# One head's relative-position scores in a fused attention stage: rotated queries against a fixed wave table in place of a skew through DRAM

## The chip, the core and the metric

The kernel runs on 1 core of one Trainium2 chip. Its engines are PE (TensorE, matrix products into PSUM), DVE (VectorE), ACT (ScalarE), POOL (GpSimd) and SP (SyncE, which here only issues DMAs). The metric is the device time of one execution in microseconds. A profiled execution gives the trace that is read below.

## What is computed

Sixteen images of 128 channels x 1024 places go through a convolution block, an attention with relative positions, and a mixture of experts. The change touches the attention alone:

```
pe = positional_encoding(S, D)                    # sin / cos of place * rate, 1024 x 128
q, k, v = (x @ W + b).reshape(B, S, H, dh)        # H = 4 heads, dh = 32
p = (pe @ Wpos).reshape(S, H, dh)
content_score = einsum('bshd,bthd->bhst', q + u_bias, k)
pos_score = rel_shift(einsum('bshd,thd->bhst', q + v_bias, p))
attn = softmax((content_score + pos_score) / sqrt(D))
out = reshape(einsum('bhst,bthd->bshd', attn, v)) @ Wout + bout

rel_shift: pad one column of zeros on the left of each S x S matrix,
           read it as (S+1) x S, drop the first row, read it as S x S
```

The shift makes row s of the position scores a copy of its unshifted row that is moved by 1023 - s places; what falls off comes from row s + 1. Within a tile of 128 query rows each row is moved by another amount.

## The kernel before

The program runs phase after phase: convolution, projection (which writes `queries`, `keys` and `values` to DRAM, each split in a high and a low part), attention, experts, and a last sum. `attention_phase` is written out by hand for each engine: five instruction queues, bound by semaphores. There is no scheduler.

An image (n) is 32 **steps** (s = 0 to 31): 8 tiles of 128 query rows, in each the 4 heads. Step s is head s % 4 of tile s // 4. Each engine goes through `slot(n, b, s)` for every step and does in it its part for this step and for some earlier ones:

- PE: `position_rows` (L1184) fills the PSUM tile `wide_ps` with 1152 columns for step s (L1173 in the trace, 3 or 4 products of up to 512 columns); `content` (L1197) fills `score_ps` for step s-5 (L1201); `turn_weights` (L1205) transposes the weights of step s-6 into `turn_ps` (L1209); every fourth step `sum_values` (L1212, at s % 4 = 2, L1219 in the trace) and the output product (s % 4 = 3, L1250).
- ACT: copies `wide_ps` to one of four `rows` tiles (L943), and takes the exponential of step s-5 in place in `skewed` (L952).
- SP: writes `rows` to DRAM (`skew_dram`, L840), and two steps later reads it back with a row pitch that is one element shorter (L849) into one of eight `skewed` tiles. This pair is the shift.
- DVE: adds `score_ps` to the shifted rows of step s-5 and takes the minimum (L1093, "reduce" below), copies `turn_ps` of step s-6 to one of eight `turned` tiles (L1101), and every fourth step scales the context (L1068), adds to `x` (L1076) and takes reciprocals (L1083, L1085).

`score_ps`, `wide_ps` and `turn_ps` are single buffers.

Beside image n runs the **routing** of image n-1 for the experts: PE transposes `x` and then the normed rows into the spare columns of `wide_ps` ahead of `position_rows` at steps 9 to 11 and 18 to 20 (`fill`, L1154), gating products at 21 (L1163) and places at 27 (L1157 to L1159); DVE does the gating at steps 22 to 25 and 28; POOL takes the root (L893), norms eight tiles (L898) and copies them (L902), which the fill of step 18 waits for (`normed`), and at the end issues 16 indirect DMAs in a row, which scatter the rows to the experts (L907). POOL has no part of the steps of image n.

## Time and profile before

| | us |
|---|---|
| median of 3 runs | 3765.72 |
| lowest, highest | 3761.39, 3768.57 |
| profiled execution, first to last instruction (span) | 4014.9 |
| first and last copy of `wide_ps` in the attention | 1316.6, 3341.0 |

The page gives no other time of the profiled execution than its span. Busy shares of the span: PE 80%, DVE 68%, ACT 55%, POOL 18%; the hardware DMA queue 70.7% of the 16 DMA engines. In the page's 40 slices the attention covers slices 14 to 34, with DMA at 8 to 9 tenths and 308 to 370 GB/s in most of them. The columns of the windows are the stretch, its length, the busy time of each engine with its count of instructions, the mean granted clock of PE as a share of full speed, the DMA share and GB/s. In a timeline a row is start, duration, engine, line, operation, out<-in, and in brackets the idle time before it with what ended it. "remote" is a releaser that the trace does not name.

### The profile page before, as it was taken

To read this page: it belongs to the slowest core of one execution; us is meant where nothing else is said; L and a number is where in the kernel's file an instruction comes from. 1 tells how busy PE (TensorE), PEld (TensorE's weight loads), DVE (VectorE), ACT (ScalarE), POOL (GpSimd) and SP (SyncE) were. 2 spreads that over 40 slices of the span, in tenths; PEclk is the share of its full clock that TensorE was granted. 3 is DMA by queue.
4 is the path that set the end of the run, shared out by engine and by line. 5 is a ranking of instruction groups with operands and counts; after the bars stand their busy time and mean duration, and the time that the engine had idled before them with its cause. 6 is when DMAs were issued, how large, how long until landed. Compare 5 with 4: busy or idle time off the path is not lost. (4 is left out here: it accounts for less than half of the span.)

```text
span 4014.9 us, 76711 instructions
## 1 busy us (share of the span) xinstructions
PE 3223.9 (80%) x29428; PEld 2425.6 (60%) x29428; DVE 2717.7 (68%) x5210; ACT 2196.9 (55%) x3568; POOL 704.4 (18%) x760
## 2 busy tenths in 40 slices
PE   4788888888566788878888888888887885799993
PEld 2556556556454576666666666667665764687772
DVE  4777877876443576668666867667666865577763
ACT  2555545545343575556655665556655652577760
POOL 1000000000001001120212112120212012466660
PEclk9899999999777898889888988888888987899995
DMA  2445545544487998899888988899888983577768
GB/s 55 143 130 176 170 119 163 181 124 167 172 292 254 323 370 309 312 322 341 315 308 313 361 314 314 306 327 345 312 304 312 354 307 129 200 236 240 238 201 335
DMA packets 290943, 1023.22 MB, mean 255 GB/s; under 512 B 51620, under 2 KB 57520, under 8 KB 281574
## 3 DMA queue, kind: packets, MB, share of 16 engines
q1 hardware_dynamic: 273382, 985.62, 70.7%
q0 software_dynamic: 17280, 33.87, 2.3%
q8 instruction: 176, 2.88, 0.3%
q14 instruction: 105, 0.86, 0.1%
HBM read 486.25 MB, written 489.85 MB: 243 GB/s over the span
## 5 line engine op out<-in xcount | busy, mean ns | idle before, releaser
L952 ACT ACTIVATE att_skewed<-att_skewed,att_neg_max 128x1024 f32<-128x1024 f32 x512 | 588.9, 1150 | 422.2 <-DVE att_neg_max L1093 419.3
L943 ACT ACTIVATE att_rows<-att_wide_ps 128x1152 f32<-128x1152 f32 x512 | 573.5, 1120 | 378.1 <-remote 240.5
L1209 PE MATMUL att_turn_ps<-att_ident,att_skewed 128*128 128x128 f32 x4096 | 610.4, 293 | 174.8 <-ACT att_skewed L952 124.2
L1209 PEld LDWEIGHTS att_turn_ps<-att_ident,att_skewed 128*128 128x128 f32 x4096 | 491.1, 150 | 370.7 <-ACT att_skewed L952 284.6
L1093 DVE CUSTOM_DVE_ANT_0 att_skewed<-att_score_ps,att_skewed 128x1024 f32<-128x1024 f32 x512 | 625.3, 1221 | 128.5 <-issue 120.1
L1101 DVE COPY att_turned<-att_turn_ps 128x1024 f32<-128x1024 f32 x512 | 624.9, 1221 | 22.4 <-PE att_turn_ps L1209 19.5
L1173 PE MATMUL att_wide_ps<-att_ps,att_qs 98*128 98x128 f32 (+3 forms) x1920 | 454.2, 358 | 32.8 <-DVE att_token L985 16.5
L1201 PE MATMUL att_score_ps<-att_ks,att_qs 96*128 96x512 f32 x1024 | 383.9, 458 | 28.9 <-DVE att_neg_max L1093 23.0
L907 POOL DMA_INDIRECT expert_rows<-att_expert_rows,att_place x256 | 247.4, 966 | 817.3 <-DVE att_place L1051 730.4
L1173 PEld LDWEIGHTS att_wide_ps<-att_ps,att_qs 98*128 98x128 f32 x1920 | 324.1, 208 | 92.3 <-issue 51.8
L1219 PE MATMUL att_tail_ps<-att_turned,att_vals 128*32 128x128 f32 x8192 | 315.7, 289 | 69.1 <-issue 66.5
L152 POOL DMA_INDIRECT expert_parts<-exp_parts,exp_rows x284 | 300.4, 1058 | 195.4 <-ACT exp_parts L183 129.4
L1219 PEld LDWEIGHTS att_tail_ps<-att_turned,att_vals 128*32 128x32 f32 x8192 | 240.5, 116 | 130.6 <-issue 126.0
L170 ACT ACTIVATE exp_hid<-exp_hid_ps,exp_weights 128x512 f32<-128x512 f32 x284 | 197.3, 695 | 133.5 <-PE exp_hid_ps L249 84.9
L1068 DVE TENSOR_TENSOR att_context<-att_tail_ps,att_recip_t 128x128 f32<-128x128 f32 x128 | 37.0, 289 | 314.6 <-remote 239.0
L1898 PE MATMUL conv_tile<-conv_stacked,conv_tap_products 128*32 128x252 f32 (+1 forms) x4608 | 223.0, 351 | 18.9 <-DMA conv_stacked<-conv_qp 18.9
L210 DVE CAST exp_hidh<-exp_hid 128x512 fp32r<-128x512 f32 x284 | 124.2, 437 | 135.5 <-ACT exp_hid L170 85.9
L1898 PEld LDWEIGHTS conv_tile<-conv_stacked,conv_tap_products 128*32 128x32 f32 x4608 | 162.5, 110 | 82.4 <-DMA conv_stacked<-conv_qp 19.3
L1201 PEld LDWEIGHTS att_score_ps<-att_ks,att_qs 96*128 96x128 f32 x1024 | 168.7, 206 | 65.6 <-DVE att_neg_max L1093 47.3
L214 DVE TENSOR_TENSOR exp_hidl<-exp_hid,exp_hidh 128x512 fp32r<-128x512 f32 x284 | 193.7, 682 | 0.0
L893 POOL TENSOR_TENSOR att_rstd<-att_var,att_minus_half 128x8 f32<-128x8 f32 x16 | 26.8, 1674 | 906.7 <-DVE att_var L1006 906.7
L1683 DVE SCALAR_TENSOR_TENSOR conv_x<-conv_x,conv_taps 128x1024 f32<-128x1024 f32 x128 | 164.5, 1285 | 4.6
(263 smaller groups left out, 5307.4 us busy)
## 6 DMA issues: line engine op xcount, KB each, us to landing
skewed_rows<-att_rows SPq DMA_DIRECT2D x512, 576.0 KB
att_skewed<-skewed_rows SPq DMA_DIRECT2D x512, 512.0 KB
expert_rows<-conv_pad SPq DMA_DIRECT2D x144, 520.0 KB, 11.0
exp_weights<-split_weights SPq DMA_DIRECT2D x71, 1028.0 KB
att_qs<-queries SPq DMA_DIRECT2D x192, 128.0 KB
att_ks<-keys SPq DMA_DIRECT2D x192, 128.0 KB
exp_rows<-expert_rows SPq DMA_DIRECT2D x71, 260.0 KB
sum_part<-expert_parts SPq DMA_DIRECT2D x32, 512.0 KB, 9.5
```

The lines of the kernel that those rows point to most:

```text
L152: pool.indirect_dma_start(parts_dram, bass.IndirectOffsetOnAxis(ap=index, axis=0), parts[b % NY][:, t, :], None, bounds_check=bound, oob_i ...
L170: act.activation(hid[:, g % NF, :], hid_ps[:, g % NH, :], ACT.Gelu, bias=bias_of(b, m)).then_inc(gelu_done, 1)
L907: pool.indirect_dma_start(rows_dram, bass.IndirectOffsetOnAxis(ap=place[k][:, t:t + 1], axis=0), expert_rows[k][:, t, :], None).then_inc(s ...
L943: act.activation(rows[s % ROWS][:], wide_ps[:, 0:WIDE], ACT.Copy).then_inc(wide_read, 1)
L952: act.activation(skewed[r % RING][:], skewed[r % RING][:], ACT.Exp, bias=neg_max[:, k:k + 1], scale=-1.0, accum_out=sums[:, k:k + 1]).then ...
L1093: dve.tensor_tensor_reduce(skewed[r % RING][:], score_ps[:], skewed[r % RING][:], -SCALE, 3.0e38, ALU.add, ALU.min, neg_max[:, k:k + 1]).t ...
L1101: dve.tensor_copy(turned[r % (2 * HEADS)][:], turn_ps[:]).then_inc(turn_read, 1)
L1173: ins = pe.matmul(bank_of[:, a:b], left, right, start=(first[a // HALF] == j), stop=(last[a // HALF] == j), skip_group_check=True)
L1201: last = pe.matmul(score_ps[:, c:c + HALF], qs[b][0:STACK, h, i * P:(i + 1) * P], ks[b][:, h, c:c + HALF], start=True, stop=True)
L1209: last = pe.transpose(turn_ps[:, t * P:(t + 1) * P], skewed[r % RING][:, t * P:(t + 1) * P], ident[:])
L1219: last = pe.matmul(tail_ps[h * DH:(h + 1) * DH, 0:P], vals[b][:, t, h, :], turned[first + h][:, t * P:(t + 1) * P], start=(t == 0), stop=( ...
L1898: last = pe.matmul(to[a * DH:(a + 1) * DH, 0:(end - rows) * WS], tap_products[:, t, a, :], stacked[:, a, rows + dy:end + dy, dx:dx + WS], ...
```

## The change

Head 0 leaves the path through DRAM. Since a sine or cosine at place a - b is a rotation of the one at a by an angle that belongs to b, the 128 rows of a tile can each be rotated by their own angle, and then multiplied with one table of waves that is the same for all rows.

- **Waves.** Once for each image, at steps 26 and 27 of the image before, PE multiplies head 0's queries with its rows of Wpos, and with these with sine and cosine exchanged, 1026 columns each, into `wide_ps` (`waves`); DVE multiplies each with a table of angles (`turn_wave`), the second into `z`; POOL adds the two at step 28 (`turn_rows`). The next fill of `wide_ps` waits for DVE (`wave_read`).
- **Each tile of head 0.** ACT makes a high part of the rotated queries (3 steps ahead), POOL the low part (2 steps ahead); PE computes 1152 columns of three products (high x high, high x low, low x high) with 128 rows instead of one product with 98; ACT copies them to one of two `direct` tiles; POOL masks the own block and the 128 columns behind, adds the two blocks and moves two columns (`mask`), and DVE waits for that (`direct_ready`) in place of the DMA.
- **DMA.** 24 pairs of write and read for each image instead of 32; three `rows` and six `skewed` tiles. Five `turned` tiles instead of eight.
- **POOL.** It now follows the steps. The root is at step 14, norming at step 16 behind the mask of that step, and the scatter is two indirect DMAs in each of eight steps, 29 to 31 of one image and 0 to 4 of the next.
- **Setup.** Four more loads, splits of the wave table and of the weights on DVE, and one round of waves ahead of the first step.

```
+            def scatter(m, t):
+                if t == 0:
+                    pool.wait_ge(normed, 2 * m + 2)
+                    pool.wait_ge(placed, m + 1)
                 for k in range(2):
-                    for t in range(TT):
-                        pool.indirect_dma_start(rows_dram, bass.IndirectOffsetOnAxis(ap=place[k][:, t:t + 1], axis=0),
-                                                expert_rows[k][:, t, :], None).then_inc(scattered, 16)
-
-            for m in range(NB):
-                route_rows(m)
+                    pool.indirect_dma_start(rows_dram, bass.IndirectOffsetOnAxis(ap=place[k][:, t:t + 1], axis=0),
+                                            expert_rows[k][:, t, :], None).then_inc(scattered, 16)
+
+            def turn_rows(n, b):
+                pool.wait_ge(wave_read, 2 * n + 2)
+                pool.tensor_tensor(rotated[b][:, :, 0:P + 1], rotated[b][:, :, 0:P + 1], crossed, ALU.add).then_inc(rotated_ready, 1)
+            def mask(n, s):
+                i = s // HEADS
+                G = TT * n + i
+                to, beyond = direct[G % 2], direct[G % 2][:, T:T + P]
+                mask_chain.begin(pool, G)
+                pool.wait_ge(wide_read, STEPS * n + s + 1)
+                mask_chain.step(pool.tensor_tensor(beyond, beyond, after_mask[:], ALU.mult))
+                mask_chain.step(pool.tensor_tensor(to[:, i * P:(i + 1) * P], to[:, i * P:(i + 1) * P], own_mask[:], ALU.mult))
+                ins = pool.tensor_tensor(to[:, i * P + 2:(i + 1) * P], to[:, i * P + 2:(i + 1) * P], beyond[:, 0:P - 2], ALU.add)
...
+            def slot(n, b, s):
+                if s < STEPS and s % HEADS == 0:
+                    mask(n, s)
+                ahead = first_ahead(n, b, s, LOW_LEAD)
+                if ahead:
+                    rotated_low(*ahead)
+                if s == TURN_ROWS_AT and not is_last(n):
+                    turn_rows(n + 1, 1 - b)
+                at = routed(n, b, s)
+                if at and at[2] == STATS_AT + 4:
+                    root(at[0])
+                if at and at[2] == OFFSET_AT + 1:
+                    route_rows(at[0])
+                if at and at[2] >= SCATTER_AT and not is_last(at[0]):
+                    scatter(at[0], at[2] - SCATTER_AT)
...
+            def turn_wave(n, b, k):
+                dve.wait_ge(wave_filled, 2 * n + k + 1)
+                to = crossed if k else rotated[b][:, :, 0:P + 1]
+                dve.tensor_tensor(to, wave_tiles, angles[:, k, :].unsqueeze(1).broadcast_to((P, TT, P + 1)), ALU.mult).then_inc(wave_read, 1)
...
                 at_least(pe, wide_read, STEPS * n + s)
+                if s - 1 in WAVES_AT and not is_last(n):
+                    pe.wait_ge(wave_read, 2 * n + 3 + WAVES_AT.index(s - 1))
                 if spared:
                     fill(*spared)
                 turn = (i + 1) * P
...
+                else:
+                    pe.wait_ge(rot_low_ready, TT * n + i + 1)
+                    pieces = [(c, d, 0, T - i * P + c) for c, d in by_bank(0, turn)]
+                    pieces += [(c, d, 1, c - i * P) for c, d in by_bank(turn, T)] + [(T, WIDE, 1, 2)]
+                    products = []
+                    for c, d, k, at in pieces:
+                        high_part, low_part = rot_high[i % 2][:, k:k + P], rot_low[i % 2][:, k:k + P]
+                        products += [(c, d, high_part, wave_high[:, at:at + d - c]), (c, d, high_part, wave_low[:, at:at + d - c]),
+                                     (c, d, low_part, wave_high[:, at:at + d - c])]
...
+                if s in WAVES_AT and not is_last(n):
+                    if s == WAVES_AT[0]:
+                        pe.wait_ge(first_loaded[1 - b], uses(n + 1, 1 - b, FIRST))
+                    pe.wait_ge(wide_read, STEPS * n + s + 1)
+                    waves(n + 1, 1 - b, WAVES_AT.index(s))
```

**PE around steps 26 to 28 of image 0.** `att_vals` marks the values of step 26, `att_context` the output product of step 27. Before:

```order
775 L1219 MATMUL att_tail_ps<-att_turned,att_vals 32x128 x32
776 L1173 MATMUL att_wide_ps<-att_ps,att_qs 128x512
777 L1173 MATMUL att_wide_ps<-att_ps,att_qs 128x384
778 L1173 MATMUL att_wide_ps<-att_ps,att_qs 128x128 x2
779 L1201 MATMUL att_score_ps<-att_ks,att_qs 128x512 x2
780 L1209 MATMUL att_turn_ps<-att_ident,att_skewed 128x128 x8
781 L1250 MATMUL att_tail_ps<-att_context,att_wout 128x128
782 L1173 MATMUL att_wide_ps<-att_ps,att_qs 128x512 x2
783 L1173 MATMUL att_wide_ps<-att_ps,att_qs 128x128
784 L1201 MATMUL att_score_ps<-att_ks,att_qs 128x512 x2
```

The same place of the program now, where the wave products stand behind the values and behind the output product (L1361), and the last rows are the start of step 28 (head 0):

```order
841 L1361 MATMUL att_wide_ps<-att_qs,att_w_wave 128x2
842 L1323 MATMUL att_wide_ps<-att_ps,att_qs 128x512
843 L1323 MATMUL att_wide_ps<-att_ps,att_qs 128x384
844 L1323 MATMUL att_wide_ps<-att_ps,att_qs 128x128 x2
845 L1368 MATMUL att_score_ps<-att_ks,att_qs 128x512 x2
846 L1376 MATMUL att_turn_ps<-att_ident,att_skewed 128x128 x8
847 L1416 MATMUL att_tail_ps<-att_context,att_wout 128x128
848 L1361 MATMUL att_wide_ps<-att_qs,att_w_wave 128x512 x2
849 L1361 MATMUL att_wide_ps<-att_qs,att_w_wave 128x2
850 L1323 MATMUL att_wide_ps<-att_wave_high,att_rot_high 128x512
851 L1323 MATMUL att_wide_ps<-att_wave_low,att_rot_high 128x512
852 L1323 MATMUL att_wide_ps<-att_wave_high,att_rot_low 128x512
```

Each run of three wave products is an extra use of `wide_ps`, between two position fills.

**DVE in steps 26 and 27 of image 0** (L1236 is the reduce, L1244 the copy of the turned weights, which stand there before as well, as L1093 and L1101), now:

```order
537 L1244 COPY att_turned<-att_turn_ps 128x1024
538 L1199 TENSOR_TENSOR att_rotated<-att_wide_ps,att_angles 128x8x129
539 L1207 TENSOR_TENSOR att_context<-att_tail_ps,att_recip_t 128x128
540 L1235 MEMSET att_marker 128x1
541 L1236 ISA att_skewed,att_neg_max<-att_score_ps,att_skewed 128x1024
542 L1236 ISA att_neg_max 128x1
543 L1244 COPY att_turned<-att_turn_ps 128x1024
544 L1199 TENSOR_TENSOR att_z<-att_wide_ps,att_angles 128x8x129
545 L1215 SCALAR_TENSOR_TENSOR att_x<-att_tail_ps,att_bias_out,att_x 128x128
```

The two rows L1199 are new; each stands behind the copy of its step.

**POOL, from one root to the next.** Before, with the whole routing of one image in four groups:

```order
44 L893 TENSOR_TENSOR att_rstd<-att_var,att_minus_half 128x8
45 L898 TENSOR_SCALAR att_expert_rows<-att_z,att_rstd,att_offset 128x128 x8
46 L902 COPY att_expert_rows<-att_expert_rows 128x8x128
47 L907 DMA expert_rows<-att_expert_rows,att_place 147456x130 x16
```

Now, from the root of step 14 to the norming of step 16, and the scatter from step 29 on:

```order
102 L947 TENSOR_TENSOR att_rstd<-att_var,att_minus_half 128x8
103 L984 TENSOR_TENSOR att_direct<-att_direct,att_after_mask 128x128
104 L985 TENSOR_TENSOR att_direct<-att_direct,att_own_mask 128x128
105 L986 TENSOR_TENSOR att_direct<-att_direct 128x126
106 L989 COPY att_direct<-att_direct 128x2
107 L954 ISA
108 L954 TENSOR_SCALAR att_expert_rows<-att_z,att_rstd,att_offset 128x128 x8
...
125 L970 TENSOR_TENSOR att_rotated<-att_rotated,att_z 128x8x129
126 L965 DMA expert_rows<-att_expert_rows,att_place 147456x130 x2
127 L975 TENSOR_TENSOR att_rot_low<-att_rotated,att_rot_high 128x129
128 L965 DMA expert_rows<-att_expert_rows,att_place 147456x130 x4
129 L984 TENSOR_TENSOR att_direct<-att_direct,att_after_mask 128x128
```

The mask of step 16 now stands ahead of the norming, and the 16 indirect DMAs are cut into pieces with masks and low parts between them.

## Rows read from the trace of the kernel before

**Rows 1.** The page's head: the profiled execution.
```profile
span 4014.9 us, 76711 instructions
```

**Rows 2.** Windows: an image without its end, a stall, a whole image (columns above).
```profile
core 0: us, PE busy (x) PEld busy (x) DVE busy (x) ACT busy (x) POOL busy (x), PEclk, DMA share, GB/s
1920.40:1938.00 17.60, 8.26 (x33) 3.90 (x32) 0.00 (x0) 0.13 (x2) 11.48 (x12) 0.56 0.43 164
1940.80:2048.00 107.20, 95.96 (x962) 76.36 (x965) 88.06 (x197) 74.00 (x109) 9.17 (x13) 0.94 0.99 355
```

**Rows 3.** Timelines of PE, DVE and POOL in a stall; POOL's first and last of 16.
```profile
1923.71 1.09 PE L1219 MATMUL att_tail_ps<-att_turned,att_vals 128*32 128x128 f32 x5 [0.86 <-issue]
1938.05 0.29 DVE L1068 TENSOR_TENSOR att_context<-att_tail_ps,att_recip_t 128x128 f32<-128x128 f32 x1 [17.66 <-remote]
1915.22 1.08 POOL L907 DMA_INDIRECT expert_rows<-att_expert_rows,att_place  x1 [49.23 <-DVE att_place L1051]
1934.28 0.96 POOL L907 DMA_INDIRECT expert_rows<-att_expert_rows,att_place  x1 [0.30 <-issue]
```

**Rows 4.** Waits: who waited for whom, us in total, times, longest.
```profile
ACT att_rows L943 <- remote: 240.5, 13, 18.7
DVE att_marker L1092 <- DMA att_skewed<-skewed_rows: 99.1, 72, 3.8
```

**Rows 5.** ACT's copies: starts of tiles 4, 5, 7 and the next image; image 8's last tile.
```profile
1991.95 1.11 ACT L943 ACTIVATE att_rows<-att_wide_ps 128x1152 f32<-128x1152 f32 x1
2006.89 1.12 ACT L943 ACTIVATE att_rows<-att_wide_ps 128x1152 f32<-128x1152 f32 x1
...
2039.85 1.11 ACT L943 ACTIVATE att_rows<-att_wide_ps 128x1152 f32<-128x1152 f32 x1
...
2069.76 1.13 ACT L943 ACTIVATE att_rows<-att_wide_ps 128x1152 f32<-128x1152 f32 x1
...
2426.37 1.11 ACT L943 ACTIVATE att_rows<-att_wide_ps 128x1152 f32<-128x1152 f32 x1
...
2439.37 1.11 ACT L943 ACTIVATE att_rows<-att_wide_ps 128x1152 f32<-128x1152 f32 x1
```

**Rows 6.** Timelines of PE and DVE through one undisturbed tile of image 5.
```profile
1950.24 0.84 PE L1173 MATMUL att_wide_ps<-att_ps,att_qs 98*128 98x128 f32 x4
1952.45 0.78 PE L1173 MATMUL att_wide_ps<-att_ps,att_qs 98*128 98x256 f32 x4
1953.07 0.68 PE L1201 MATMUL att_score_ps<-att_ks,att_qs 96*128 96x512 f32 x2
1954.21 1.09 PE L1209 MATMUL att_turn_ps<-att_ident,att_skewed 128*128 128x128 f32 x8 [0.46 <-ACT att_skewed L952]
1959.65 1.09 PE L1209 MATMUL att_turn_ps<-att_ident,att_skewed 128*128 128x128 f32 x8 [0.54 <-ACT att_skewed L952]
1962.56 0.81 PE L1173 MATMUL att_wide_ps<-att_ps,att_qs 98*128 98x256 f32 x4
1951.64 1.22 DVE L1093 CUSTOM_DVE_ANT_0 att_skewed<-att_score_ps,att_skewed 128x1024 f32<-128x1024 f32 x1 [0.97 <-issue]
1954.19 1.22 DVE L1093 CUSTOM_DVE_ANT_0 att_skewed<-att_score_ps,att_skewed 128x1024 f32<-128x1024 f32 x1
1957.09 1.22 DVE L1093 CUSTOM_DVE_ANT_0 att_skewed<-att_score_ps,att_skewed 128x1024 f32<-128x1024 f32 x1
```

**Rows 7.** Timelines: POOL's norming, PE's fill that needs it, and a DVE product with PSUM.
```profile
1992.09 3.46 POOL L898 TENSOR_SCALAR att_expert_rows<-att_z,att_rstd,att_offset 128x128 f32<-128x128 f32 x8 [4.38 <-DVE att_offset L1058]
1995.76 0.52 PE L1154 MATMUL att_wide_ps<-att_ident,att_expert_rows 128*128 128x128 f32 x3
1100.94 1.21 DVE L579 TENSOR_TENSOR proj_zl<-proj_z_ps,proj_zh 128x1024 fp32r<-128x1024 f32 x1
```

**Rows 8.** DMA issues: the two transfers of the shift.
```profile
skewed_rows<-att_rows SPq DMA_DIRECT2D x512, 576.0 KB
att_skewed<-skewed_rows SPq DMA_DIRECT2D x512, 512.0 KB
```

239 lines of the change are left out of this document (177 added, 62 removed).

## The prediction

> **What bounds the kernel now.** Three views, in this order: the windows and the waits, to split the attention in kinds of stretches; ACT's copies of `wide_ps`, one for each step, as a clock of the program; and the timelines of PE and DVE through one tile, to see which chain sets its length.
>
> The first thing to see is a stall that comes once for each routed image. While POOL issues its 16 indirect DMAs in a row (from 1915.22 to 1935.2), PE gets its instructions in driblets, DVE sits 17.66 us, DMA falls to 0.43 [rows 2, 3]. It makes the last tile of an image 29.9 us (2039.85 to 2069.76) where image 8, whose stall comes later, has 13.0 [rows 5]: 16.9 us, in 15 images 254 us. 13 of them show as ACT waits of together 240.5 us [rows 4]. Now the span is 4014.9 [rows 1], and 4014.9 - 254 = 3761, which is the timed median within 5 us. I read this as a stall that only the profiled execution has. The sum is therefore made against the span without it, 3761, and carried over to 3765.7; the other reading is a rival below.
>
> Image 5 runs from 1940.8 (the window's start) to 2069.76, 129.0 us, less the stall 112 [rows 2, 5]. An undisturbed tile takes 12.32 (PE's fills at 1950.24 and 1962.56, [rows 6]). What sets it is a chain: reduce of step 0 (1954.19), exponential, reciprocal, reduce of step 1 (1957.09), exponential, transposes (1959.65), values, fill of step 3 (1962.56), content, reduce of step 3, copy, add, reduce of step 0. PE waits 0.46 and 0.54 in it [rows 6]. So PE is not the bound by its throughput, but three quarters of what it does there stands on the chain or close to it. DVE waits for the read-back 99.1 us in all [rows 4], 6.2 for each image, mostly in tiles 4 and 5, with the DMA share at 0.99 [rows 2].
>
> **The change part by part.**
>
> *Head 0's products.* The fill of step 0 took 0.62 us (1952.45 to 1953.07, [rows 6]) for 1152 columns in one product; three products of the same pieces take 1.88, so +1.26 for each tile. Where does it go? Content of step 0 was issued at 1953.07 and DVE can reduce 0.72 later (1950.92 to 1951.64 in the step before), at 1953.79, but DVE came only at 1954.19 [rows 6]: slack 0.40. With the longer fill content is issued at 1954.33, the reduce starts at 1955.05: +0.86 to 0.88 on the chain. If both PE waits of the tile take it up, 1.26 - 1.00 = 0.26 is left; if none, 1.26. I take 0.88, from the rows of the chain itself: x 128 tiles = **+113** (33 to 161).
>
> *Waves.* At step 26 PE has done the values; the three wave products take about 0.55 (1026 columns at 0.62 for 1152), DVE's product of PSUM with a table 1.15 (start to next start; 1.21 in the row of the same form, [rows 7]), hand-overs 0.4, and the fill of step 27 waits for it, on the chain: +2.1. At step 27 the wave products hide behind DVE's copy of the turned weights, but DVE's product does not, and behind it stand PE's fill of step 28 (now 1.88) and content before DVE can reduce again: 1.15 + 0.1 + 1.88 + 0.72 = 3.85 where 0.27 stood (the add: 2.55 from reduce to reduce [rows 6], less reduce and copy of 1.14 each, their 1.22 overlapping the next), +3.6, of which 0.88 is counted above: +2.7. Together 4.8 x 15 = **+72**. Below, only the two DVE products count (2 x 1.15, 35); above, half of the exposed part more (98).
>
> *Norming.* POOL's eight operations take 3.46 [rows 7], the last ending at 1995.55, and PE's fill of step 18 starts at 1995.76: just in time. Now they stand behind the mask of step 16. From the start T of the fill of step 16: fill and copy to T + 3.2, mask (three products of 128 columns, no row of this form; 0.43 each by the one-input form of the norming, 0.6 at most with two inputs, and three hand-overs and a small copy) 2.2 more, norming to T + 8.9. PE is there at T + 6.2. It waits 2.7, of which some 0.7 of slack ahead of the transposes is to be taken off, and its own fill of about 0.3 (0.52 in its row, overlapping the next) added: 2.35 x 15 = **+35** (0 to 50). Who waits for PE there is the whole chain.
>
> *DMA.* Of each image's 32 pairs of 576 and 512 KB [rows 8] eight go: 8.9 of some 41.4 MB (35.7 of pairs, 5.8 of loads, stores and scatter). At 355 GB/s [rows 2] what is left takes 92 of 112 us, so I expect DVE's waits for the read-back to go. They are 6.2 an image; what a tile gains is less, since next in line is the chain: tile 4 took 14.94 (1991.95 to 2006.89, [rows 5]), and without the wait 12.32 and 0.6 of fills. That is 2.0, tile 5 about 1. In the timed runs the DMA queues have no stall in which to catch up, so I go nearer to the whole: 5 x 16 = **-80** (-30 to -99).
>
> *Scatter, root, high parts, fewer buffers: 0.* POOL in steps 29 to 36 has 16 x 1.26 (0.96 and 0.30 between them, [rows 3]) = 20.2, two masks 4.4, the addition of the waves about 2.3 and two low parts 1: 28 us in eight steps of 29 or more. It keeps up, barely; the reduce needs the mask only five steps after its fill, which is the cover. If POOL fell a step behind, PE would wait for the low part. ACT's part (129 columns of a copy once a tile) lies in its waits. The wait for a `turned` tile has always been met by PE's order.
>
> *Setup:* the first waves, the addition and the parts, one after the other, and 3.5 us of splits beside the position DMAs: **+9** (5 to 15).
>
> Sum: 113 + 72 + 35 - 80 + 9 = +149, so 3765.7 + 149 = **3915**.
>
> **The rivals.**
>
> *A, the stalls are real.* If the burst of 16 indirect DMAs starves PE in the timed runs too, spreading it over eight steps, with 1.26 us bites that PE's queue can ride out (the first DMA is at 1915.22, the stall begins at 1920.4, [rows 2, 3]), gives back up to 254 us: 3765.7 + 149 - 254 = 3661, and with a third of it left 3745; the middle is **3700**, faster. It decides if more than 149 of the 254 is really there. Against: it leaves the 249 us between span and median without a place. 12%.
>
> *B, the DMA is the whole bound.* Share 0.99 at 355 GB/s between stalls [rows 2]; 41.4 MB at that rate are 117 us, more than an image's 112, so the chain might be as long as it is only because the data comes so. Then PE's new work fills time in which it waited for data anyway, and all waits go: 0 + 35 + 0 - 99 + 5 = -59, **3707**, faster. The Trainium skill ("SBUF — State Buffer", section "Summary: rules for kernel authors") gives about 358 GB/s as what HBM allows between HBM and SBUF; the trace's 355 agrees, and by that rule the change takes work off the engine that binds, and should pay. Against: tiles with no DMA wait at all stand at 12.3, on the chain of rows 6. 7%.
>
> *C, the clock.* In each image the granted clock averages 0.94, not 1 [rows 2]; it falls after pauses of PE. Norming and waves add three pauses of 1.5 to 2.7 us an image, and the longest fill follows two of them. If it runs at 1.2 instead of 2.4 GHz it takes 1.9 more, with the transposes and values beside it some 4 an image: **3975**. The Trainium skill ("TensorE: Matmul & The Clock Gate", section "What's actually happening") says the slow clock is the default and activity lifts it, which would make this the likelier. 8%.
>
> *D, the change doesn't do what it says:* DVE waits as long as before, now for POOL's masks behind the scatter instead of for read-backs, and nothing of the 80 is gained: 3765.7 + 229 = **3995**. 3%.
>
> **How the numbers follow.** Forecast 3915, 70%, its own range 3820 to 4010 by the bounds of its terms taken not all at once. A 12%, B 7%, C 8%, D 3%. The range goes from 3760 to 4030: it holds the forecast, C and D, and leaves A, B and a thin tail out, some 20%. Faster than 3758 (0.2%, about what a measurement can tell here): A and B less their upper ends, 0.17; within 0.2%: 0.03, the forecast's lowest end; slower: 0.80.
>
> **What would show it.** In the profile after: tile length in the first tiles 13.2 instead of 12.3; a pause of PE of 2 to 3 us ahead of the fill of step 18, ended by POOL; two pauses ended by DVE's wave products at steps 27 and 28, with the last tiles the longest; no waits of DVE for read-backs; and a span whose stalls are gone or smeared, so that the profiled execution may well be shorter than before while the timed one is longer. Wrong: tiles of 12.3 or less (B), a timed gain near the stalls' sum (A), DVE waiting for `direct_ready`, or PE for low parts (POOL overloaded, which nothing above prices).

## The result, and the profile after

| | before | after |
|---|---|---|
| median, us | 3767.14 (4 runs) | 4024.8 (4 runs) |
| lowest, highest | 3761.39, 3773.73 | 4021.52, 4032.01 |
| span of the profiled execution | 4014.9 | 4030.1 |

The ratio is 1.0689, with a 95% interval of 1.0672 to 1.0705: the change makes the kernel about 260 us slower (253 to 266). The forecast was 149 slower, and its own range of 3820 to 4010 ends below the 4024.8. The direction was right, and so was the kind of cost of each part of the change; but two terms came out at half or less of what was measured, and one cost had no term. One of 17 further executions of the kernel before (5771.1 us) and one of the six of the run without head 0's transfers (4550.7 us) had a granted clock of 0.49 and 0.61 throughout, and no ratio below uses them.

The page of the kernel after: its head, the busy times, and the hardware DMA queue (queue, packets, MB, share of the 16 engines' span).

```profile
span 4030.1 us, 79404 instructions
...
PE 3331.7 (83%) x30486; PEld 2622.4 (65%) x30486; DVE 2794.0 (69%) x5251; ACT 2239.7 (56%) x3696; POOL 997.3 (25%) x1416
...
q1 hardware_dynamic: 236662, 842.89, 62.8%
```

Span and median now agree within 6 us, while they stood 248 apart before [rows 1]: the stalls behind POOL's burst of indirect DMAs [rows 2, 3] are gone, and no wait of the trace ends in "remote" any more. And the transfers are fewer: 842.89 MB where the kernel before had 985.62. The waits for the read-back [rows 4] have shrunk to this (who waited for whom, us in total, times, longest):

```profile
DVE att_marker L1235 <- DMA att_skewed<-skewed_rows: 0.2, 1, 0.2
```

So all that the change was to take away, it took. What it costs shows in the windows of one image, cut at ACT's copies into its eight tiles (stretch, length, busy time of each engine with its instructions, granted clock of PE, DMA share, GB/s):

```profile
core 0: us, PE busy (x) PEld busy (x) DVE busy (x) ACT busy (x) POOL busy (x), PEclk, DMA share, GB/s
2082.40:2095.50 13.10, 12.05 (x132) 10.14 (x131) 10.36 (x20) 9.54 (x15) 9.53 (x13) 1.00 0.85 289
2095.50:2108.70 13.20, 12.11 (x132) 10.14 (x131) 10.39 (x20) 9.65 (x15) 4.17 (x8) 1.00 0.84 276
...
2135.50:2154.40 18.90, 16.08 (x141) 13.56 (x140) 10.43 (x20) 10.74 (x18) 6.44 (x14) 0.82 0.73 249
2154.40:2169.30 14.90, 14.79 (x147) 13.37 (x146) 12.05 (x25) 9.96 (x16) 1.98 (x5) 0.89 0.82 275
2169.30:2194.70 25.40, 20.10 (x141) 16.18 (x141) 16.69 (x38) 9.91 (x16) 1.93 (x5) 0.76 0.66 224
2194.70:2212.10 17.40, 14.38 (x130) 11.36 (x130) 13.15 (x27) 9.54 (x15) 10.26 (x12) 0.87 0.46 160
```

The plain tiles last 13.1 to 13.2, where the one of [rows 6] had 12.3. Tile 4 (norming), tile 6 and tile 7 (waves) carry most of the loss, and in them the granted clock is 0.76 to 0.87, with 1.00 in the plain tiles. For tile 6 that is no new thing: in the kernel before it stands at 0.81 there (last section of the experiments). The DMA share, 0.99 before [rows 2], is 0.46 to 0.85 in these rows: nobody waits for the DMA now, and what it has gained in room is not used.

Since ACT's copies of `wide_ps` are a clock of the program, the mean length of each tile over images 1 to 14 can be set side by side for every kernel. That of the kernel before is read from the run of it without the stalls (spread, below).

| us a tile | 0 | 1 | 2 | 3 | 4 | 5 | 6 | 7 | image |
|---|---|---|---|---|---|---|---|---|---|
| before, scatter spread | 13.0 | 12.7 | 12.5 | 13.1 | 15.2 | 14.9 | 17.9 | 13.0 | 112.4 |
| after | 13.1 | 13.2 | 13.4 | 13.5 | 18.7 | 15.0 | 25.3 | 17.6 | 129.7 |
| norming first | 13.1 | 13.2 | 13.4 | 13.5 | 14.8 | 14.2 | 22.8 | 18.0 | 123.0 |
| addition first | 13.1 | 13.2 | 13.4 | 13.5 | 16.7 | 14.3 | 25.4 | 14.5 | 124.0 |
| one product | 12.3 | 12.3 | 12.5 | 13.1 | 17.3 | 14.3 | 22.6 | 17.0 | 121.4 |
| no waves | 13.1 | 13.2 | 13.4 | 13.4 | 18.8 | 14.9 | 18.3 | 14.1 | 119.3 |
| PE kept busy at 18 | 13.1 | 13.2 | 13.4 | 13.5 | 16.0 | 14.7 | 24.4 | 18.0 | 126.3 |
| both first | 13.1 | 13.2 | 13.4 | 13.5 | 14.8 | 14.3 | 22.6 | 14.8 | 119.7 |
| both first, PE kept busy | 13.1 | 13.2 | 13.4 | 13.5 | 14.8 | 14.5 | 21.2 | 14.0 | 117.7 |
| both first, a wave early | 13.1 | 13.2 | 13.4 | 16.3 | 14.6 | 14.9 | 20.2 | 14.0 | 119.6 |
| before, no DMA for head 0 | 12.3 | 12.3 | 12.5 | 13.1 | 13.2 | 14.5 | 18.0 | 13.0 | 108.8 |

### The profile page after: what moved, and what is told of

Same layout as the page of the kernel before. It is cut to its first block and busy times, and to the rows that moved or that the text cites. A ratio compares the mean times of both kernels' runs of the same rounds, so it can differ in the third digit from the quotient of the medians.

```text
span 4030.1 us, 79404 instructions
## 1 busy us (share of the span) xinstructions
PE 3331.7 (83%) x30486; PEld 2622.4 (65%) x30486; DVE 2794.0 (69%) x5251; ACT 2239.7 (56%) x3696; POOL 997.3 (25%) x1416
## 3 DMA queue, kind: packets, MB, share of 16 engines
q1 hardware_dynamic: 236662, 842.89, 62.8%
## 5 line engine op out<-in xcount | busy, mean ns | idle before, releaser
L1236 DVE CUSTOM_DVE_ANT_0 att_skewed<-att_score_ps,att_skewed 128x1024 f32<-128x1024 f32 x384 | 468.2, 1219 | 335.6 <-issue 335.0
L1244 DVE COPY att_turned<-att_turn_ps 128x1024 f32<-128x1024 f32 x512 | 624.7, 1220 | 41.0 <-PE att_turn_ps L1376 40.8
L1070 ACT ACTIVATE att_skewed<-att_skewed,att_neg_max 128x1024 f32<-128x1024 f32 x384 | 441.8, 1150 | 220.6 <-DVE att_neg_max L1236 220.6
L1061 ACT ACTIVATE att_rows<-att_wide_ps 128x1152 f32<-128x1152 f32 x384 | 430.8, 1122 | 115.1 <-PE att_wide_ps L1323 115.0
L1376 PE MATMUL att_turn_ps<-att_ident,att_skewed 128*128 128x128 f32 x3072 | 431.3, 286 | 58.1 <-ACT att_skewed L1070 57.4
L1376 PEld LDWEIGHTS att_turn_ps<-att_ident,att_skewed 128*128 128x128 f32 x3072 | 376.3, 148 | 150.5 <-ACT att_skewed L1070 108.2
L1323 PE MATMUL att_wide_ps<-att_ps,att_qs 98*128 98x128 f32 (+3 forms) x1440 | 343.2, 362 | 7.0 <-ACT att_rows L1061 3.1
L1323 PEld LDWEIGHTS att_wide_ps<-att_ps,att_qs 98*128 98x128 f32 x1440 | 246.4, 210 | 46.5 <-issue 17.7
L1070 ACT ACTIVATE att_direct<-att_direct,att_neg_max 128x1024 f32<-128x1024 f32 x128 | 147.2, 1150 | 152.9 <-DVE att_neg_max L1236 152.9
L1061 ACT ACTIVATE att_direct<-att_wide_ps 128x1152 f32<-128x1152 f32 x128 | 145.2, 1135 | 110.7 <-PE att_wide_ps L1323 110.7
L1376 PE MATMUL att_turn_ps<-att_ident,att_direct 128*128 128x128 f32 x1024 | 178.2, 331 | 33.0 <-ACT att_direct L1070 32.0
```

The lines of the kernel that those rows point to most:

```text
L1061: act.activation(to[:], wide_ps[:, 0:WIDE], ACT.Copy).then_inc(wide_read, 1)
L1070: act.activation(weights(m, r), weights(m, r), ACT.Exp, bias=neg_max[:, k:k + 1], scale=-1.0, accum_out=sums[:, k:k + 1]).then_inc(exps_do ...
L1236: dve.tensor_tensor_reduce(weights(m, r), score_ps[:], weights(m, r), -SCALE, 3.0e38, ALU.add, ALU.min, neg_max[:, k:k + 1]).then_inc(scor ...
L1244: dve.tensor_copy(turned_at(m, r)[:], turn_ps[:]).then_inc(turn_read, 1)
L1323: ins = pe.matmul(bank_of[:, a:b], left, right, start=(first[a // HALF] == j), stop=(last[a // HALF] == j), skip_group_check=True)
L1376: last = pe.transpose(turn_ps[:, t * P:(t + 1) * P], weights(m, r)[:, t * P:(t + 1) * P], ident[:])
```

## The experiments

Each is given with its ratio to the kernel before, run on the same chip; differences are taken between ratios, at 3767 us for 1, and are good to 10 to 13 us. The table above is of one profiled execution each.

### Norming ahead of the mask

The first theory after the trace was that the pause for POOL costs twice: as a wait, and through the clock. PE and POOL of the kernel after at step 16 to 18 (start, duration, engine, line, out<-in, idle time before with its releaser):

```profile
2136.66 0.46 POOL L984 TENSOR_TENSOR att_direct<-att_direct,att_after_mask 128x128 f32<-128x128 f32 x1 [5.75 <-ACT att_direct L1061]
...
2138.38 3.52 POOL L954 TENSOR_SCALAR att_expert_rows<-att_z,att_rstd,att_offset 128x128 f32<-128x128 f32 x8
...
2142.05 0.87 PE L1304 MATMUL att_wide_ps<-att_ident,att_expert_rows 128*128 128x128 f32 x3 [2.27 <-POOL att_expert_rows L954]
2142.57 1.42 PE L1323 MATMUL att_wide_ps<-att_ps,att_qs 98*128 98x512 f32 x4
2143.79 1.16 PE L1368 MATMUL att_score_ps<-att_ks,att_qs 96*128 96x512 f32 x2
2144.75 1.91 PE L1376 MATMUL att_turn_ps<-att_ident,att_direct 128*128 128x128 f32 x8
2146.58 2.69 PE L1385 MATMUL att_tail_ps<-att_turned,att_vals 128*32 128x128 f32 x64
```

The pause of 2.27 lies in the 2 to 3 us that the prediction gave for it, in the place it named. Behind it the fill, content, transposes and values take 1.42, 1.16, 1.91 and 2.69; with the clock at full the same instructions take 0.83, 0.68, 1.04 and 1.95 (rows of the next experiment).

```diff
@@ POOL, slot(n, b, s)
+                at = routed(n, b, s)
+                if at and at[2] == OFFSET_AT + 1:
+                    route_rows(at[0])
                 if s < STEPS and s % HEADS == 0:
                     mask(n, s)
 ...
-                if at and at[2] == OFFSET_AT + 1:
-                    route_rows(at[0])
```

> The changed kernel, with POOL's norming (eight products and a copy) put ahead of the mask of step 16 instead of behind it; the computation is the same. The forecast's term (PE waits 2.35 us an image for the norming, 15 images, 35 us): 4025 - 35 = 3990. Theory after the trace of the changed kernel (the pause also lowers PE's clock for the fill, transposes and values behind it; tile 4 lasts 18.9 us where the first image's, without routing, has 13.1 and the kernel before has 14.9): tile 4 falls to about 15, 4 us in each of 15 images less 0.5 for the mask now later: 4025 - 55 = 3970, between 3960 and 3980. If the reduce now waits for the mask (it has five steps), nothing is gained: 4025.

Measured: 3941.38 us, ratio 1.0449 (1.0427 to 1.0472), so 90 us back, more than the 55 expected. Tile 4 falls from 18.7 to 14.8 as the theory said, tile 5 by 0.8, and tile 6, two tiles on and untouched by the edit, by 2.5, which the expectation had not counted. The clock in tiles 4 and 5 is back at 1.00 (windows of image 8, tiles 4 to 6):

```profile
2356.35:2371.16 14.81, 13.63 (x141) 11.16 (x141) 11.07 (x20) 10.55 (x17) 6.00 (x14) 1.00 0.92 319
2371.16:2385.24 14.08, 13.51 (x147) 11.83 (x146) 12.13 (x25) 9.75 (x17) 1.96 (x5) 1.00 0.91 295
2385.24:2407.94 22.70, 17.23 (x141) 13.89 (x141) 16.52 (x38) 9.90 (x17) 1.92 (x5) 0.85 0.67 213
```

### PE kept busy in the same pause

This leaves the wait where it is and takes away only its effect on the clock.

```diff
@@ PE, fill(m, b, r)
                 if r == NORMED_AT:
+                    for _ in range(4):
+                        for c in (0, HALF):
+                            pe.matmul(wide_ps[:, c:c + HALF], rot_high[0][:, 0:P], wave_high[:, c:c + HALF], start=True, stop=True)
                     pe.wait_ge(normed, 2 * m + 1)
```

> The changed kernel, with PE doing eight products of 512 columns into the free wide_ps in the pause of step 18, in which it otherwise waits for POOL's norming (added work without use; it is overwritten). Theory (clock): the pause stays, but the fill, transposes and values behind it run at the full clock (0.9, 0.9 and 0.7 us shorter), tile 4 falls from 18.9 to 16.1, and tile 6 gains something of its own as with the norming ahead: 4025 - 50 = 3975, between 3940 and 3985. Rival (only the pause itself costs): no gain, 4025, or slower if the added products outlast the pause.

Measured: 3978.58 us, ratio 1.0542 (1.0515 to 1.0570), so 55 us back, with eight useless products more. Timeline of PE at step 18 in it:

```profile
2001.54 2.13 PE L1303 MATMUL att_wide_ps<-att_wave_high,att_rot_high 128*128 128x512 f32 x8
2003.89 0.55 PE L1308 MATMUL att_wide_ps<-att_ident,att_expert_rows 128*128 128x128 f32 x3 [0.22 <-POOL att_expert_rows L955]
2004.19 0.83 PE L1327 MATMUL att_wide_ps<-att_ps,att_qs 98*128 98x512 f32 x4
2004.86 0.68 PE L1372 MATMUL att_score_ps<-att_ks,att_qs 96*128 96x512 f32 x2
2005.38 1.04 PE L1380 MATMUL att_turn_ps<-att_ident,att_direct 128*128 128x128 f32 x8
2006.35 1.95 PE L1389 MATMUL att_tail_ps<-att_turned,att_vals 128*32 128x128 f32 x64
```

PE still goes on only when POOL has normed (the last 0.22 of the pause are left), and everything behind it is at its short duration. Tile 4 has 16.0, with the granted clock at 1.00 in all images. The 55 us come back although POOL's norming ends no sooner, so they are the clock's. What the wait itself costs its tile is the step from 14.8 (norming first) to 16.0, 1.2 us or 18 us in all; the rest of the 35 that separate this run from norming first is in tiles 5 and 6, which are 0.5 and 1.6 longer here, and at a lower clock (0.92 and 0.80 in the mean of the images, against 0.99 and 0.86). The wait stayed and the clock was given back, which shows the clock's part apart from the wait's.

### The addition of the waves ahead of the mask

The kernel after has a row that nothing had prepared for. DVE, POOL and PE at step 28 and 29:

```profile
2197.65 2.37 POOL L970 TENSOR_TENSOR att_rotated<-att_rotated,att_z 128x1032 f32<-128x1032 f32 x1
...
2197.99 2.06 DVE L1178 TENSOR_SCALAR att_token<-att_token 128x8 f32<-128x8 f32 x1
...
2201.36 0.33 PE L1408 MATMUL att_tail_ps<-att_ident,att_recip 128*128 128x128 f32 x1 [2.00 <-DVE att_recip L1224]
```

A DVE instruction on eight numbers a partition lasts 2.06 us, and ends when POOL's addition ends. The reciprocal is behind it, and PE stands 2.00.

```diff
@@ POOL, slot(n, b, s)
+                if s == TURN_ROWS_AT and not is_last(n):
+                    turn_rows(n + 1, 1 - b)
                 if s < STEPS and s % HEADS == 0:
                     mask(n, s)
 ...
-                if s == TURN_ROWS_AT and not is_last(n):
-                    turn_rows(n + 1, 1 - b)
```

> The changed kernel, with POOL's addition of the two wave products (128x1032, 2.37 us) put ahead of the mask of step 28 instead of behind it; the computation is the same. It then runs while DVE waits for PE's long fill. Theory (port): DVE's update of the token numbers, 128x8, took 2.06 us instead of 0.16 exactly while POOL's addition ran, and PE then waited 2.0 us for DVE's reciprocal and lost its clock: about 2 to 3 us in each of 15 images, 4025 - 38 = 3987, and the token update is back at 0.16 us. Rival (that instruction is slow because of what it reads, not because of POOL): 4025 and still 2 us. Rival (the mask, now 2.4 us later, is waited for): 4025 or above.

Measured: 3956.78 us, ratio 1.0486 (1.0464 to 1.0507), so 76 us back, twice what was expected. The groups of that instruction (line, shape, count, busy us, mean ns, idle before), of the kernel before, of after and of this run, in this order:

```profile
L1044 DVE TENSOR_SCALAR att_token<-att_token 128x8 f32<-128x8 f32 x16 | 2.6, 161 | 0.8 <-ACT att_positions L924 0.8
```
```profile
L1178 DVE TENSOR_SCALAR att_token<-att_token 128x8 f32<-128x8 f32 x16 | 26.8, 1673 | 0.8 <-ACT att_positions L1039 0.8
```
```profile
L1178 DVE TENSOR_SCALAR att_token<-att_token 128x8 f32<-128x8 f32 x16 | 2.6, 162 | 0.8 <-ACT att_positions L1039 0.8
```

1673 ns go back to 162 by moving POOL's instruction, with nothing changed on DVE. Tile 7 loses 3.1 of its 17.6 us, 15 times, 46 us. The longer instruction explains at most 1.9 of the 3.1; the rest goes with the granted clock of the tile, 0.86 before and 0.97 after the edit. The other part of the gain is in tiles 4 and 5 (18.7 to 16.7, 15.0 to 14.3), which the edit doesn't touch: in 9 of 14 images tile 4 has 16.0 to 16.1, the length that the run with PE kept busy has, although the pause of the norming is as before. Image 8 is one of the nine (PE behind the pause, and the window of the tile):

```profile
2373.52 0.52 PE L1304 MATMUL att_wide_ps<-att_ident,att_expert_rows 128*128 128x128 f32 x3 [2.25 <-POOL att_expert_rows L954]
2373.79 0.83 PE L1323 MATMUL att_wide_ps<-att_ps,att_qs 98*128 98x512 f32 x4
```
```profile
2366.94:2383.01 16.07, 13.27 (x141) 11.23 (x141) 10.34 (x20) 10.79 (x18) 6.42 (x14) 1.00 0.83 290
```

So the same pause can leave the clock at full. In the other five images it is 0.82 to 0.90 in this tile. Why nine go one way and five the other no run shows. The nine also confirm the price of the wait alone: 16.0 against 14.8.

The Trainium skill ("SBUF — State Buffer", section "Who interferes with whom") states that when a DVE instruction in a mode that uses both ports and a GpSimd instruction meet, the one issued first has the shared ports for its whole length and the other is blocked. The rows agree: POOL's started 0.34 us earlier, and DVE's ends with it. In which mode DVE ran the instruction no row tells.

### Both together

> The changed kernel with both orders on POOL turned round: norming ahead of the mask of step 16 and the addition of the waves ahead of the mask of step 28. Alone they gave 83 and 68 us. If they are separate: 4025 - 83 - 45 = 3897 (tile 7's 2.9 us come on top, the gain of tile 4 in the second is the same as in the first): tiles 4 to 7 14.8, 14.1, 22.8, 14.5. If both gains come from one clock effect: 3940.

Measured: 3907.03 us, ratio 1.0361 (1.0333 to 1.0388), so 124 us of the 260 back, less than 90 + 76, since both had counted the clock of tiles 4 and 5. Tiles 4 to 7 are at 14.8, 14.3, 22.6 and 14.8, as expected. Two pieces of POOL's work in another order are worth half of the loss.

### One product instead of three

```diff
@@ PE, position_rows, head 0
-                        high_part, low_part = rot_high[i % 2][:, k:k + P], rot_low[i % 2][:, k:k + P]
-                        products += [(c, d, high_part, wave_high[:, at:at + d - c]), (c, d, high_part, wave_low[:, at:at + d - c]),
-                                     (c, d, low_part, wave_high[:, at:at + d - c])]
+                        high_part = rot_high[i % 2][:, k:k + P]
+                        products += [(c, d, high_part, wave_high[:, at:at + d - c])]
```

> The changed kernel with one product instead of three for each piece of head 0's position scores (it leaves out the two correction products; POOL still makes the low parts and the waits stay). The forecast's term (0.88 a tile, 128 tiles, 113): 4025 - 113 = 3912. If the clock makes it dearer where the fill follows a pause (step 28, 2.66 us instead of 1.9, and step 16): 3895. If the DMA is the whole bound: 4025.

Measured: 3900.02 us, ratio 1.0339 (1.0316 to 1.0362), so 132 us, 1.03 a tile. Tiles 0 to 2 fall from 13.1 to 13.4 back to 12.3 to 12.5, 0.8 to 0.9 each: the chain of [rows 6] held there. What goes beyond 0.88 is tile 6, with 2.7, and tile 4, with 1.4. For tile 6, two rows show why: the first of the nine products of step 28's fill, and the content behind it, in the kernel after, in the version with both orders turned and PE kept busy ahead of this fill (next section), and in the run with the norming first.

```profile
2191.85 0.47 PE L1323 MATMUL att_wide_ps<-att_wave_high,att_rot_high 128*128 128x512 f32 x1 [1.81 <-issue]
...
2194.51 1.16 PE L1368 MATMUL att_score_ps<-att_ks,att_qs 96*128 96x512 f32 x2
```
```profile
2359.59 0.50 PE L1327 MATMUL att_wide_ps<-att_wave_high,att_rot_high 128*128 128x512 f32 x1
...
2361.37 0.71 PE L1374 MATMUL att_score_ps<-att_ks,att_qs 96*128 96x512 f32 x2
```
```profile
2405.97 0.47 PE L1323 MATMUL att_wide_ps<-att_wave_high,att_rot_high 128*128 128x512 f32 x1 [2.07 <-issue]
...
2407.74 0.68 PE L1368 MATMUL att_score_ps<-att_ks,att_qs 96*128 96x512 f32 x2
```

The same fill takes 2.66 us behind a pause of 1.81 and 1.78 us behind work. But in the third it takes 1.77 behind a pause of 2.07: what sets its length is the granted clock, and a pause just ahead lowers that in some images and runs and not in others. In the kernel after, tile 6 has the lowest mean clock of all tiles, and the dear fill was put there.

### No waves, and the waves' price in two parts

```diff
@@ POOL, ACT
-                if s == TURN_ROWS_AT and not is_last(n):
-                    turn_rows(n + 1, 1 - b)
-                pool.tensor_tensor(rot_low[k][:, 0:P + 1], rotated[b][:, i, 0:P + 1], ...)
+                pool.tensor_tensor(rot_low[k][:, 0:P + 1], rotated[0][:, i, 0:P + 1], ...)
-                act.activation(rot_high[i % 2][:, 0:P + 1], rotated[b][:, i, 0:P + 1], ...)
+                act.activation(rot_high[i % 2][:, 0:P + 1], rotated[0][:, i, 0:P + 1], ...)
@@ DVE
-                if s in WAVES_AT and not is_last(n):
-                    turn_wave(n + 1, 1 - b, WAVES_AT.index(s))
@@ PE
-                if s - 1 in WAVES_AT and not is_last(n):
-                    pe.wait_ge(wave_read, 2 * n + 3 + WAVES_AT.index(s - 1))
 ...
-                    waves(n + 1, 1 - b, WAVES_AT.index(s))
```

> The changed kernel with the wave products made for the first image alone (leaves out, for images 1 to 15, PE's wave products, DVE's two products with the angle tables and POOL's addition; all images use the first one's rotated queries). The forecast's term (4.8 us an image, 15 images, 72): 4025 - 72 = 3953. Theory after the trace: tile 6 lasts 25.4 us with waves and 18.3 in the last image, which has none, 7.1; tile 7 17.3 where 13.2 is a plain one and some routing stays, 2 to 4: together 9 to 11, 4025 - 150 = 3875, between 3860 and 3890.

Measured: 3880.57 us, ratio 1.0284 (1.0262 to 1.0306), so 153 us: twice the forecast's term, and what the tiles had said. Tile 6 goes from 25.3 to 18.3 and tile 7 from 17.6 to 14.1. To split this, PE was given transposes of the identity in three pauses, on top of both orders on POOL:

```diff
@@ PE, position_rows
                 if s - 1 in WAVES_AT and not is_last(n):
+                    pe.wait_ge(turn_read, STEPS * n + s - TURN_LAG)
+                    busy(8, turn_ps)
                     pe.wait_ge(wave_read, 2 * n + 3 + WAVES_AT.index(s - 1))
@@ PE, slot, last_of_tile(n, b, s, TURN_LAG)
+                    if s == 25 and not is_first(n):
+                        busy(10, tail_ps)
                     pe.wait_ge(recip_ready, G + 1)
```

> The changed kernel with both POOL orders turned round (3907), and added products without use in three pauses of PE: ten transposes at step 25, eight each ahead of its waits for DVE's two wave products (into turn_ps, once DVE has read it, so they run beside the wave product). It splits the waves' price of 144 us in waiting and clock. Theory: the pauses stay, the fills, content, transposes and values behind them run at the full clock, tile 6 falls from 22.8 to about 20.3 and tile 7 from 14.7 to 14: 3907 - 48 = 3859 (3845 to 3885). Rival (the price is the waiting alone): 3907.

Measured: 3870.09 us, ratio 1.0268 (1.0248 to 1.0288), 35 us under the kernel with both orders turned. Tile 6 of image 8, first without and then with the added transposes:

```profile
2356.83:2379.64 22.81, 16.55 (x141) 13.31 (x141) 16.52 (x38) 9.89 (x17) 4.34 (x6) 0.89 0.67 221
```
```profile
2340.72:2361.57 20.85, 17.87 (x167) 14.54 (x167) 16.51 (x38) 9.89 (x17) 3.87 (x6) 1.00 0.71 236
```

26 more instructions on PE, 1.3 us more busy, and a tile shorter by 2. So of the 153 us some 46 are the collision of tile 7 with the clock behind it, and up to 35 the clock (a part of the 35 belongs to the gating's pause at step 25, which the kernel before has too). About 72 are left for the waiting. That this is the forecast's term says little: it is a difference of four runs, good to some 17 us, and not a run of its own.

### A wave at an earlier step

```diff
-WAVES_AT = (26, 27)
+WAVES_AT = (14, 26)
```

> The changed kernel with both POOL orders turned round (3907), and the two wave products at steps 14 and 26 instead of 26 and 27; the computation is the same. Theory (each wave takes wide_ps from the chain for about 2.1 us and has its price anywhere, but beside the gating two pauses follow each other and the clock stays low): tile 3 grows from 13.4 to 16, tiles 6 and 7 lose 4: 3907 - 20 = 3887 (3875 to 3900). Rival (the price is that of the place alone: next to the gating and the values): 3907 - 55 = 3850. Rival (the same price anywhere): 3907.

Measured: 3883.19 us, ratio 1.0309 (1.0287 to 1.0330), 20 us under both orders alone. Tile 3 grows by 2.8, tiles 6 and 7 lose 3.2 together. A wave has its price anywhere; next to another pause a little more, if at all: the tile means shift by tenths in other places too (tile 5 +0.6), and the mean image of the profiled execution is 119.6 where both orders alone had 119.7 in their fastest. The 20 us, good to 13, are all that speaks for the place.

### The kernel before, without head 0's transfers

Its write to DRAM and its read-back are left out, with the waits of DVE and ACT for them, and the reduce adds what stands in the buffer.

```diff
@@ SP, slot(n, b, s)
-                if s < STEPS:
+                if s < STEPS and s % HEADS:
 ...
-                if before:
+                if before and before[2] % HEADS:
@@ DVE, slot, S_LAG
+                    if r % HEADS:
-                    dve.wait_ge(skew_landed[r % RING], ...)
+                        dve.wait_ge(skew_landed[r % RING], ...)
```

> The kernel before, with head 0's write to DRAM and its skewed read-back left out (its reduce adds what stands in the buffer; everything else as before). It prices what the change takes off the DMA, alone. The forecast's term: -80 (-30 to -99), so 3767 - 80 = 3687. Rival, from the tiles measured since (tile 4 lasts 14.8 us without the norming pause, as in the kernel before, although two short products more are in it): the waits went, but the next in line ends almost as late, 1 to 3 us an image, so -15 to -50: 3735.

Measured: 3708.61 us, ratio 0.9835 (0.9810 to 0.9861), 62 us faster. The forecast's 80 was too much, the rival's 15 to 50 too little. Tile 4 loses 2.0 as the prediction worked out, tile 5 0.4 where it had about 1, and tiles 0 and 1 0.7 and 0.4. DVE's waits for the read-back in this run, in the kernel before with its scatter spread, and in the version with the gating moved (below):

```profile
DVE att_marker L1095 <- DMA att_skewed<-skewed_rows: 25.1, 20, 3.5
```
```profile
DVE att_marker L1094 <- DMA att_skewed<-skewed_rows: 124.7, 117, 3.7
```
```profile
DVE att_marker L1092 <- DMA att_skewed<-skewed_rows: 149.7, 128, 5.9
```

### The kernel before, with its scatter spread

```diff
@@ POOL, route_rows
-                for k in range(2):
-                    for t in range(TT):
+                for t in range(TT):
+                    if m < NB - 1:
+                        pool.wait_ge(wide_read, min(STEPS * (m + 1) + 29 + t, STEPS * NB))
+                    for k in range(2):
                         pool.indirect_dma_start(...)
```

> The kernel before, with POOL's 16 indirect DMAs of an image spread over eight steps (two for each, released by the copies of steps 29 to 36) instead of one burst; the computation is the same. The forecast held the 250 us stall to be the profiled execution's alone: timed 3767 as before, within 0.3%, while the profiled span falls from 4015 to about 3765. Rival A (the stalls are real): timed 3515 to 3700.

Measured: 3763.16 us, ratio 0.9990 (0.9972 to 1.0009): the same. The head of its page:

```profile
span 3757.7 us, 76711 instructions
```

The span fell by 257 us and the time by nothing. The stall belongs to the profiled execution with a burst of indirect DMAs, and rival A with it.

### Two versions of the kernel before

At step 25 PE waits for a reciprocal behind the gating in the kernel before too (this row is of its spread run), and tile 6 is at a clock of 0.81 there (first window below).

```profile
2513.31 0.33 PE L1244 MATMUL att_tail_ps<-att_ident,att_recip 128*128 128x128 f32 x1 [1.47 <-DVE att_recip L1087]
```

```diff
@@ PE, slot, last_of_tile(n, b, s, TURN_LAG)
+                    if s == 25 and not is_first(n):
+                        for _ in range(10):
+                            pe.transpose(tail_ps[:, 3 * P:4 * P], ident[:], ident[:])
                     pe.wait_ge(recip_ready, G + 1)
```

> The kernel before, with ten transposes of the identity into free columns of tail_ps in PE's pause of step 25 of each routed image (1.47 us, in which it waits for DVE's reciprocal behind the gating); added work without use. Behind that pause the granted clock is 0.66 to 0.78 in the kernel before too, and the fill takes 1.28 instead of 0.83 us, content 1.22 instead of 0.67, the transposes 1.97 instead of 1.04, the values 2.78 instead of 1.95. Theory (clock): 2.7 us an image given back, 3767 - 40 = 3727 (3715 to 3745). Rival (the clock falls for another reason than the pause, or DVE sets the tile): 3767.

Measured: 3755.18 us, ratio 0.9964 (0.9945 to 0.9982), 14 us. Then the gating itself one step later:

```diff
-GATES_AT = (22, 23, 24, 25, 28)
+GATES_AT = (22, 23, 25, 26, 28)
```

> The kernel before, with the third and fourth part of the gating one step later on DVE (steps 25 and 26 instead of 24 and 25), so that the reciprocal of step 25 comes ahead of them; the computation is the same. Theory: the pause of 1.47 us and its clock both go, tile 6 falls from 18.4 to about 15: 3767 - 50 = 3717 (3700 to 3745). Rival (the pause moves with the gating to step 26, ahead of the values, context or reduce): 3767 within 10.

Measured: 3745.31 us, ratio 0.9929 (0.9904 to 0.9954), 27 us faster: under one per cent, but a version that beats both kernels, by one line of numbers. Tile 6 of an image in the spread run, in the first version and in the second:

```profile
2506.93:2525.31 18.38, 15.34 (x128) 12.09 (x128) 14.52 (x38) 9.58 (x17) 0.00 (x0) 0.81 0.92 341
```
```profile
2285.58:2301.90 16.32, 13.51 (x138) 10.80 (x138) 14.54 (x38) 9.58 (x17) 0.00 (x0) 1.00 1.02 370
```
```profile
2287.25:2302.36 15.11, 12.68 (x128) 9.71 (x128) 14.46 (x38) 9.46 (x16) 0.00 (x0) 1.00 1.03 375
```

Both do to this tile what was expected: 18.4, 16.3, 15.1, with the clock at 1.00. Over images 1 to 14 the means are 17.9, 16.7 and 15.3; in the first version five of the 14 images still have 0.80 to 0.90 there. And the time moves by 14 and 27 where 40 and 50 were expected: the DMA share is now 1.02 in these rows, and DVE's waits for the read-back rise from 124.7 in the spread run to 149.7 in the second version (rows above). Its tiles 6 save 2.6 x 15 = 39, and its tiles 0 and 5 are 1.3 and 0.5 longer.

## Why the prediction was right, and where it was not

**The stall and the base of the sum.** Right, and the step on which most hung: the sum was made against a span without stalls. Taken as real, the burst would have led to 3700.

**How near it was.** The measured 4024.8 lies above the forecast's own range (3820 to 4010) and above both dearer rivals, C (3975) and D (3995), and 5 us inside the widest range, which had been drawn to 4030 to hold them. That it still lies inside is luck: no term or rival gave such a time.

**Head 0's products: 113 forecast, 132 measured, inside 33 to 161.** The slack argument held to a tenth in tiles 0 to 2: the fill lasts 1.77 instead of 0.62 and the tile 0.8 to 0.9 longer (0.3 in tile 3). What goes beyond is in tiles 4 and 6, whose clock is low, where the term had taken 0.88 as everywhere.

**DMA: -80 forecast, -62 measured.** In the kernel after the waits did go, all but 0.2 us; in the run that gives the 62 they fell from 124.7 to 25.1. "I go nearer to the whole" was the step that failed by 18: a wait that goes is worth less than its length, as the next in line is the chain.

**Norming: 35 forecast, with 0 to 50 as its range; 90 measured.** The pause is 2.27 where 2.7 was worked out, and at full clock it costs its tile 1.2 and not 2.35. So the wait was priced too high, and the clock, which made most of the 90, not at all: it was put to rival C, as a case of its own at 8%, and not to the term. The rows for it were there: in the kernel before the granted clock averaged 0.94 [rows 2].

**Waves: 72 forecast, with 35 to 98; 153 measured.** (The 98 doesn't follow from its words: half of 72 more is 108.) The same step failed again, for up to 35 us, and another cost had no term at all: "Scatter, root, high parts, fewer buffers: 0" asked only if POOL keeps up, and never if POOL and DVE can work at once. The addition of the waves was costed at nothing beside other work, and cost 46 us in its own tile and 76 in all.

**Setup: 9 forecast.** The first copy of the attention comes at 1323.1, and at 1311.1 in the spread run: 12. But it comes at 1316.6 in the kernel before itself, and at up to 1333.0 in the variants of the kernel after, so this term is known to some 6 us at best.

**The sum.** The terms as measured one by one make 132 + 90 + 153 - 62 + 12 = 325, not 260. They overlap, mostly in tile 6: norming first, one product and no waves take 2.5, 2.7 and 7.0 from it, together 12.2, where it is only 7.4 longer than before. Each of them also gives back clock there and counts it for itself. No run takes all the terms away at once.

**The rivals.** A fell by the spread run. C was not a rival but an addition: its mechanism is shown, with up to 90 us (55 and 35) of the loss where it had 60. Its sizes were otherwise: in the rows shown the dear fill takes 0.9 more and not 1.9, and the trace has four new pauses and not three, the fourth being the 2.00 that PE waits for the reciprocal while POOL adds the waves. The Trainium skill ("TensorE: Matmul & The Clock Gate", section "What's actually happening") has the slow clock as the default that activity lifts, and the two runs of the kernel after with added work agree, with 1.00 in all images of tile 4 and in 11 of 14 of tile 6. D didn't come: the last operation of a mask ends at least 11.8 us ahead of the reduce that needs it, in all 128 tiles. B fell for the change, but it tells something true of the kernel before: in its spread run and its two versions of the last section the mean image of the profiled execution stays at 112.4, 112.0 and 111.6, at a DMA share up to 1.03, and without head 0's transfers it is 108.8. The change freed the DMA, and spent on the chain some five times what that was worth (260 + 62 against 62).

**What would show it** came out as listed: tiles of 13.1 to 13.2, a pause of 2.27 ended by POOL ahead of step 18's fill, no waits for read-backs, a profiled span nearly as before. The two pauses at steps 27 and 28 are there too, with 1.38 and 1.81; the trace doesn't name DVE as what ends them, but the run without waves has neither.

## What to carry to other kernels

A pause of PE is priced with what runs behind it: read the durations of the same instructions at either clock, and put the difference in the term, not in a rival. It is an upper bound, since the clock doesn't fall behind every pause. Work that is moved to an idle engine needs two questions, if that engine keeps up and if another engine can run beside it; where not, an order of two instructions may be worth more than the instruction. And before a transfer is traded for engine work, see how much of the transfer is exposed: here 62 us, against more than 250 on the chain.

## What the hardware showed that was not expected

- A DVE instruction of 0.16 us took 2.06 while POOL added two SBUF tiles, and 0.16 again when POOL's was moved.
- Pauses of 1.4 to 2.3 us often had the granted clock at half behind them, and eight products of 512 columns, or eight to ten transposes, in them raised it: to 1.00 in tile 4 of all images, in tile 6 of 11 of 14 (kernel after, both orders turned) and of 9 of 14 (kernel before). But pauses of 2.07 and 2.25 also stood ahead of work at full clock.
- The same program meets different clocks from image to image. The images of the run with PE kept busy repeat in threes from image 6 on, 126.9, 128.3 and 123.9 us long, and tile 4 of the run with the addition first has 16.0 to 16.1 in most images and 17.6 to 18.8 in the others.
- The clock can be at half without a pause ahead of it. Steps 20 and 21 of the kernel after:

```profile
2154.39:2158.32 3.93, 3.82 (x31) 3.46 (x30) 2.77 (x6) 2.49 (x6) 1.51 (x4) 1.00 1.00 342
2158.32:2161.72 3.40, 3.40 (x16) 3.12 (x15) 2.40 (x4) 2.72 (x6) 0.00 (x0) 0.51 0.58 189
```

PE is busy all through. With the norming first it stays at 1.00 in most images, so it could be a late effect of that pause. But the kernel before without head 0's transfers has no such pause, and has the same in its tile 5 (image 8):

```profile
2228.00:2238.73 10.73, 10.51 (x125) 8.87 (x124) 7.03 (x15) 7.54 (x13) 0.00 (x0) 1.00 0.93 340
2238.73:2242.15 3.42, 3.42 (x16) 3.22 (x15) 2.45 (x4) 2.75 (x5) 0.00 (x0) 0.50 0.93 265
```

Why the clock falls there no run tells, and it stays open.
